# Moving the issue of the c-row loads from SyncE's step to the end of ScalarE's step

## The reference, cut to what matters

```
gate = x Wg' + 0.5 (x Ag[id]') Bg[id]'      up = likewise with Wu, Au, Bu
act  = silu(gate) * up
down = act Wd' + 0.5 (act Ad[id]') Bd[id]'
x1   = x + down sign(W0)' + bias0
out  = x1 + ffn1(16/16 * (x1 B[id2]') A[id2]')
ffn1(z) = z (W1 + 2 sum_n w_n lora_B_n lora_A_n)' + bias1
```

## Time and profile before

| | us |
|---|---|
| median of 3 runs | 895.37 (895.09 to 895.53) |
| the profiled execution, its own time | 896.58 |
| its span in the profile | 894.8 |
| PE busy | 889.5 (99%) |
| DVE busy | 411.1 (46%) |
| ACT busy | 203.8 (23%) |
| POOL busy | 122.1 (14%) |
| granted PE clock, all 40 slices | 9 tenths or more |

### The profile page before, as it was taken

The page is one execution under the profiler, slowest core; times in us unless marked ns, Lnnn a source line. Parts: engine busy times, 40 slices in busy tenths (PEclk is TensorE's granted clock), DMA queues, the critical chain, the costliest instruction groups (busy, mean ns, idle before and its releaser), DMA issues.

```text
span 894.8 us, 22056 instructions
## 1 busy us (share of the span) xinstructions
PE 889.5 (99%) x7567; PEld 732.7 (82%) x7567; DVE 411.1 (46%) x986; ACT 203.8 (23%) x381; POOL 122.1 (14%) x141
## 2 busy tenths in 40 slices
PE   9999999999999999999999999999999999999998
PEld 6888888888888888888888888888888888888885
DVE  5854444444343544434444443444444435354443
ACT  4852212212121211211212222121221212121110
POOL 0200111010111111011111011111101011111111
PEclk9999999999999999999999999999999999999999
DMA  9934454554555455455545545555555555555543
GB/s 340 418 116 135 125 156 135 151 148 131 161 139 147 137 149 150 138 151 148 145 136 148 152 144 136 157 137 153 136 150 147 133 159 140 155 131 146 151 120 91
DMA packets 148947, 137.33 MB, mean 153 GB/s; under 512 B 54848, under 2 KB 120384, under 8 KB 148800
## 3 DMA queue, kind: packets, MB, share of 16 engines
q1 hardware_dynamic: 93696, 111.24, 43.3%
q10 hardware_dynamic: 54288, 22.70, 9.7%
q0 software_dynamic: 944, 3.15, 0.9%
HBM read 94.80 MB, written 11.01 MB: 118 GB/s over the span
## 4 chain that ended last, share of the span: by engine, by line
PE 98%; DVE 1%; DMA 0%; ACT 0%; issue 0%; SPq 0%; DVEq 0%
PE gu_ps L849 56%; PE y_ps L886 27%; PE out_ps L908 3%; PE gu_ps L994 3%; PE out_ps L959 2%; PE gu_ps L985 1%; PE out_ps L895 1%; PE y_ps L849 1%; PE out_ps L849 1%; PE out_ps L916 1%; PE gu_ps L886 1%; DMA lb_raw<-in_lbw 0%; DVE a_lo L635 0%; PE gu_ps L1023 0%; DVE weff_raw L781 0%
## 5 line engine op out<-in xcount | busy, mean ns | idle before, releaser
L849 PE MATMUL gu_ps<-wu_sb,xT_sb 128*128 128x432 f32 (+1 forms) x1152 | 261.2, 371 | 0.0
L849 PE MATMUL gu_ps<-wg_sb,xT_sb 128*128 128x432 f32 (+1 forms) x1152 | 254.6, 370 | 0.5 <-DVE act_all L653 0.5
L886 PE MATMUL y_ps<-down_sb,actT_sb 128*128 128x512 f32 x1023 | 242.3, 394 | 0.0
L886 PEld LDWEIGHTS y_ps<-down_sb,actT_sb 128*128 128x128 f32 x1023 | 189.7, 188 | 60.9 <-issue 21.4
L849 PEld LDWEIGHTS gu_ps<-wg_sb,xT_sb 128*128 128x128 f32 x1152 | 216.5, 188 | 25.8 <-DVE xT_sb L635 1.4
L849 PEld LDWEIGHTS gu_ps<-wu_sb,xT_sb 128*128 128x128 f32 x1152 | 214.1, 188 | 21.3 <-issue 0.3
L635 DVE TENSOR_TENSOR actT_sb<-landed,actT_sb 128x512 fp32r<-128x512 f32 (+1 forms) x96 | 60.7, 633 | 193.6 <-ACT actT_sb L484 193.6
L484 ACT CAST actT_sb<-landed 128x512 fp32r<-128x512 f32 (+1 forms) x96 | 56.1, 585 | 311.2 <-DMA landed<-act_all 199.5
L443 POOL TENSOR_TENSOR x_in<-x_in,bias_sb 128x512 f32<-128x512 f32 x32 | 41.2, 1288 | 615.8 <-DMA x_in<-in_x 615.8
L635 DVE TENSOR_TENSOR xT_sb<-xT_raw,xT_sb 128x512 fp32r<-128x512 f32 x32 | 22.1, 691 | 105.1 <-ACT xT_sb L484 105.1
L667 DVE TENSOR_TENSOR t_own<-out_ps,const_sb 128x64 f32<-128x64 f32 x32 | 7.2, 225 | 135.6 <-PE out_ps L908 133.2
(11 more groups left out here) (125 smaller groups left out, 559.6 us busy)
## 6 DMA issues: line engine op xcount, KB each, us to landing
b_rows<-in_btab SPq DMA_DIRECT2D x128, 236.0 KB, 3.1
a_raw<-in_atab SPq DMA_DIRECT2D x128, 152.0 KB, 2.3
landed<-act_all SPq DMA_DIRECT2D x132, 64.0 KB, 2.1
xT_raw<-in_xT SPq DMA_DIRECT2D x32, 256.0 KB, 2.6
x_in<-in_x SPq DMA_DIRECT2D x32, 256.0 KB, 2.8
landed<-act_all ACTq DMA_DIRECT2D x124, 64.0 KB, 2.2
x_landed<-x_turn ACTq DMA_DIRECT2D x124, 64.0 KB, 2.2
out_x<-out_sb SPq DMA_DIRECT2D x31, 256.0 KB, 3.0
```

Source lines behind the costliest of these rows:

```text
L849: last = nc.tensor.matmul(o, w, m, start=start and n == 0, stop=stop and n == len(terms) - 1, skip_group_check=not check)
L886: last = nc.tensor.matmul(to[:], actT_sb[:, ACTT_SLOT[c] + n, a, :], down_sb[:, blk, b, :], start=begin and (c, n) == (0, 0) and (a, b) == ...
```

## The change

The four c-row loads of steps 1 to 30 leave SP's step, where they stood between the third chunk's send and the B-row loads, and are issued by ACT at the very end of its step, behind the `split_actT` of the third chunk. `row_of` and `load_c` take the engine as an argument; the last step's c loads stay on SP. In steps 1 to 30 the destination, the source, the sizes and the semaphore stay the same.

```diff
+        def row_of(engine, ids, g, b, count):
+            return nc.values_load(idx_feat[0:1, ids, bass.ds(g * GB + b, 1)], engines=[engine], min_val=0,
+                                  max_val=(count - 1) * P,
...
+        def load_c(engine, on, g, batch=range(GB), to=2, signal=L["c_in"]):
+            for b in batch:
+                at = row_of(on, 1, g, b, R1)
+                rows, n = low_rows(b, to)
+                engine.dma_start(cs_rows[rows, n, :], c_view[bass.ds(at, P), :].rearrange("(r e) w -> r (e w)", e=8)
+                                 ).then_inc(signal, 16)
...
@@ sync, step @@
                 if last(g):
-                    load_c(prev, range(0, 2))
+                    load_c(sp, SP, prev, range(0, 2))
...
                 else:
                     load_sbd(g)
                     send_act(sp, g, 2)
-                    if prev is not None:
-                        load_c(prev)
                     load_b(nxt)
@@ scalar, step @@
                 if prev is not None:
                     send_x1(act, prev)
                 split_actT(g, 2)
+                if prev is not None and not last(g):
+                    load_c(act, ON_ACT, prev)
```

More of the change, by code:

```diff
@@ L283, in send_x1 @@
             send(engine, x1_landed, x1_turn, H, L["x1T_in"], range(4))
+        def row_of(engine, ids, g, b, count):
+            return nc.values_load(idx_feat[0:1, ids, bass.ds(g * GB + b, 1)], engines=[engine], min_val=0,
+                                  max_val=(count - 1) * P,
+                                  skip_runtime_bounds_check_because="the ids are clamped on the chip")
+        def load_c(engine, on, g, batch=range(GB), to=2, signal=L["c_in"]):
[4 more added lines that the diff above has]
+                                 ).then_inc(signal, 16)
         def columns(half):
@@ L296, in rows_stored @@
                 engine.wait_ge(rows_free[k], 16 * len(range(k, 10, ROWS_RING)))
+        SP, ON_ACT = mybir.EngineType.SP, mybir.EngineType.Activation
         @block.sync
@@ L328, in _ @@
             sp.dma_start(xT_raw[:], xT[0:P, :].rearrange("p (k t) -> p k t", k=KC)).then_inc(L["xT_in"], 16)
[L330 to L333, removed]
             def load_a(g):
                 for b in range(GB):
-                    at = row_of(0, g, b, R0)
+                    at = row_of(SP, 0, g, b, R0)
                     sp.dma_start(a_raw[:, b, :], atab[bass.ds(at, P), :]).then_inc(L["a_in"], 16)
@@ L350, in load_b1 @@
                 for b in range(GB):
-                    at = row_of(1, g, b, R1)
+                    at = row_of(SP, 1, g, b, R1)
                     sp.dma_start(b1_raw[:, b, :], b1tab[bass.ds(at, P), :]).then_inc(L["b1_in"], 16)
@@ L361, in load_sbd @@
                                  ).then_inc(L["sbd_in"], 16)
[L363 to L368, removed]
             sp.wait_ge(S["ids_done"], 2)
@@ L399, in step @@
                 else:
-                    load_c(g, range(GB), 1, E["c_in"])
+                    load_c(sp, SP, g, range(GB), 1, E["c_in"])
                 if prev is not None:
@@ L411, in step @@
                     load_sbd(g)
-                    load_c(prev, range(2, GB))
+                    load_c(sp, SP, prev, range(2, GB))
                     load_b1end(g)
```

## The result

The changed kernel takes 909.81 us (median of 6 runs, 906.16 to 913.08) against 895.33 us before: 1.0163 times as long, 95% interval 1.0151 to 1.0174, or 14.5 us more. The forecast was 895.4 and no change. The runs after also spread over 7 us, where the kernel before spreads over 0.44. (The table of the kernel before gives 895.37 from three runs; 895.33 is the median of six.) The profiled execution is the quickest of the six, 906.16 us with a span of 904.1, so it shows 9.3 us of the loss.

What follows compares the result with a forecast made beforehand. PE, busy 25.89 of each 25.89 us step, was taken to bound the kernel; 30 steps x 0, plus 0 at the start and 0 in the tail, left 895.37 + 0, rounded 895.4 us, range 894.3 to 896.8.

Steps and rivals of the forecast that it cites:

- What bounds the kernel, and the question asked of it: Loop step: PE busy 25.89 of 25.89 us; the question was how much room lies ahead of each PE wait.
- the tightest margin: PE's mid-up wait for the x1 sends: previously landed by 519.8, wanted at about 521.7, room 1.9 us.
- ScalarE: ACT before `move_ad`: four c loads take 3.3 us of 5.14 us idle, bounds 1.3 to 5.5; cost 0.
- I take 3.0 us under load, so the last lands at 520.6, 1.1 us ahead of PE's wait. Cost 0: Last x1 send beside the earlier B loads: 3.0 us to landing, bounds 2.0 and 4.3, cost 0.
- the 521.7 that I worked out: Middle of up: PE wants the x1 sends after three of six matmuls, minus the weight load, at about 521.7.
- the bound of 4.3: Longest landing of such sends in the whole earlier run, taken as upper bound: x1 late by 0.2 us.
- the trace of before neither shows nor excludes the collision: Said of B on SP's queue taking about every second turn from ACT's x1 sends, at most doubling their landing.
- Rival 1: x1 arrives late beside B, deciding from 4.1 us landing; 901.4 us at 4.3, 904.4 at 4.4; chance 0.05.
- At most double: x1 sends beside B: queues taking turns by packet would at most double the 2.2 us landing, to 4.4.
- The c rows: Issued by ACT from 519 to 522.2, landed by 524.7, wanted at 529.7, 5.0 us later; cost 0.
- B's own arrival: B loads issued from about 515.3 instead of 518.50, wanted at 529.7, room already 4.7 us; arriving earlier worth 0.
- the tail: Last step: SP's work starts about 3.2 us earlier until the store at 868.79 waits for DVE; gains 0.

Runs made afterwards that it cites:

- b_waits_x1: Changed kernel, but SP issues the first B-row load only when the turned x1 has landed; 895.41 us, ratio 1.0000 to the kernel before.
- its repeat: The changed kernel measured once more, nothing altered, beside other runs on the same chip; 909.92 us, ratio 1.0145 to the kernel before.
- the later wait: Changed kernel with PE's wait for the turned x1 and its small products one quarter of up later; 899.51 us, ratio 1.0032 to the kernel before.
- Half the bytes: Changed kernel, each B-row load from step 2 on moving 472 of 944 columns, as many DMAs; 895.73 us, ratio 1.0001 to the kernel before.

## Why the prediction was wrong, point by point

**What bounds the kernel, and the question asked of it: right.** Time could only be lost by something arriving late at one of PE's waits, and the tightest margin was rightly named: the last x1 send at `small_ready`.

**ScalarE: right.** Four loads were put at 3.3 us, about 2.8 from the first issue to the end of the fourth; they take 2.91, in the idle time ahead of `move_ad`, which PE still ends. `b_waits_x1` prices this part at 0.

**Wrong: the term "I take 3.0 us under load, so the last lands at 520.6, 1.1 us ahead of PE's wait. Cost 0".** The fourth send takes 4.1 us on average in the changed kernel (3.4 to 5.0 in the loop) and 4.5 in its repeat. Two smaller terms go the same way. The sends themselves are issued more slowly beside B, 2.75 us for four in the step shown in place of 2.53, so the last goes out later, by 0.1 us on average. And PE stands from 521.6 on, not from the 521.7 that I worked out. In the changed kernel the last send goes out 3.6 us behind `add_y` on average, so the room from its issue is 7.43 - 3.61 = 3.8 us, where I had 4.1. A send that lands early gives nothing back, so the size comes from the late steps alone: 9.8 us over the 28 of the loop in the trace that lost 9.3.

The pick of 3.0 was the error, not the mechanism: the bound of 4.3 that the earlier trace rows gave stood beside it, and between 3.0 and 4.3 lay the whole result. Those 4.3 us were no stray value either. They are the last x1 send of step 1 in the trace of before, and what it met is B, whose first load came 1.0 us behind the first send there (SyncE, ScalarE, then the landing of the last two sends):

```profile
102.25 3.88 SPq L344 DMA_DIRECT2D b_rows<-in_btab  x4
...
101.22 2.54 ACTq L274 DMA_DIRECT2D x_landed<-x_turn  x4
...
DMA to landing us min/median/max: 3.0/3.7/4.3
```

So the sentence that the trace of before neither shows nor excludes the collision is wrong: it held one, and a landing stretched to 4.3 by it. It shows no clear price, since step 1 took 26.05 us there and 25.97 in the changed kernel, where that send landed in 3.2. Rival 1 had the mechanism, the place and the point of decision, and 901.4 to 904.4 us, too little still; it got a chance of 0.05.

**"At most double": too low for single sends.** By the Trainium skill, "DMA: Bandwidth & Descriptors", section "Queues, rings and completion order", I capped the stretch at twice the landing. The means stay near it, 2.3 to 4.1 and 4.5, but single fourth sends reached 5.0 and 5.2, and 5.6 with the later wait, 2.5 times the 2.25 of before. A turn there is a packet, so equal turns needn't be equal time, and my step from turns to "double" took them as equal. Here a piece of B keeps a DMA engine busy for 214 ns on average and one of an x1 send for about 28. That this difference is the whole of the excess is argued, not shown. What the page's section "Issuing engines are not separate DMA queues" says, that issuing from another engine saves sequencer time alone, agrees with `b_waits_x1`: with B held back, the move itself gives a ratio of 1.0000.

**The c rows, B's own arrival and the tail: right.** No wait of PE names any of them, and the loss sits in the loop's steps.

## What to carry to other kernels

When a load leaves a queue, ask first what stood behind it there: it moves up, and its bytes land on whatever is in flight at its new time; the moved load itself may cost nothing. A margin of one transfer against a wait has to be reckoned with that transfer's landing under the new neighbour, for the last of a row of sends and not for their median, and where the trace holds both a quiet and a loaded landing, the loaded one is the one to take. A wait on a semaphore that holds the neighbour back until the urgent transfer has landed gave all of the time back here.

## What was not expected of the hardware

B loads that come a little after the first urgent send hurt the last one no less than those that come with it: its mean landing was 4.5 and 4.6 us with B 0.4 to 0.5 us behind, and 4.1, 4.3 and 4.5 with B 0.2 to 0.4 us ahead. That they hurt more isn't shown, since those kernels ran on different chips and the intervals of their times overlap. Half the bytes cut the added landing of the last send from 1.9 us (4.12 less 2.25) to 0.4 (2.66 less 2.25), by far more than half. And ScalarE's id read runs beside its own cast: the first c load is issued at 313.85, before the cast that started at 313.28 ends at 313.90.
